# Four fused image layers on one core: channel-group means by block turns on VectorE for the later images, with new orders on all engines

## The reference, cut to what matters

```python
# L1: G = 32 groups of 4 channels, eps 1e-6;  L2: G = 16 groups of 8 channels, eps 1e-5
xg = x.reshape(B, H, W, G, C // G)
mean = jnp.mean(xg, axis=(1, 2, 4), keepdims=True)
var = jnp.var(xg, axis=(1, 2, 4), keepdims=True)
xn = (xg - mean) * jax.lax.rsqrt(var + EPS)
```

## Time and profile before

| | |
|---|---|
| median of 3 runs | 160.66 us (159.46 to 163.44) |
| the profiled execution | 159.53 us, of which the core's span is 157.7 us |
| PE, weight loads | busy 149.7 us (95%), 114.7 us (73%) |
| DVE, ACT, POOL | busy 104.8 us (66%), 108.7 us (69%), 50.1 us (32%) |
| granted clock of PE | full in all slices |

### The profile page before, as it was taken

How to read it: one execution, slowest core, us unless ns; L and a number is a source line. 1 busy time by engine, 2 the same in 40 slices (tenths; PEclk the granted TensorE clock), 3 DMA queues, 4 the chain that set the end, 5 groups by cost and what they waited for, 6 DMA issues and landing times.

```text
span 157.7 us, 3715 instructions
## 1 busy us (share of the span) xinstructions
PE 149.7 (95%) x1405; PEld 114.7 (73%) x1405; DVE 104.8 (66%) x265; ACT 108.7 (69%) x261; POOL 50.1 (32%) x115
## 2 busy tenths in 40 slices
PE   7989999999999999999989997999989999999992
PEld 4569889887777678766667765766677756799992
DVE  0577899999996898568956377639975611235543
ACT  3567979973688458983778942697358879567970
POOL 6467657534517442214020038010200050026100
PEclk9999999999999999999999999999999999999999
DMA  5960000000000000000000000000000020000003
GB/s 147 321 267 0 0 8 0 2 4 0 2 2 4 0 0 4 4 0 4 4 2 6 4 0 0 8 0 4 2 2 8 0 75 0 0 4 33 0 33 133
DMA packets 2800, 4.30 MB, mean 27 GB/s; under 512 B 352, under 2 KB 2272, under 8 KB 2784
## 3 DMA queue, kind: packets, MB, share of 16 engines
q1 hardware_dynamic: 2496, 3.87, 7.2%
q10 hardware_dynamic: 288, 0.21, 0.4%
HBM read 2.90 MB, written 1.05 MB: 25 GB/s over the span
## 4 chain that ended last, share of the span: by engine, by line
PE 71%; DVE 16%; ACT 5%; POOL 4%; issue 2%; DVEq 0%; ACTq 0%
PE psum L658 9%; PE psum L647 8%; PE psum L626 7%; DVE nmax L1148 6%; PE psum L573 4%; PE psum L553 3%; PE psum L685 3%; PE psum L699 3%; ACT pT L907 3%; PE psum L728 3%; PE psum L669 2%; PE psum L721 2%; PE psum L720 2%; PE psum L518 2%; PE psum L737 2%
## 5 line engine op out<-in xcount | busy, mean ns | idle before, releaser
L1148 DVE TENSOR_REDUCE nmax<-psum 128x4 f32<-128x1024 f32 x32 | 38.3, 1217 | 6.7 <-PE psum L626 6.7
L907 ACT ACTIVATE pT<-psum 128x1024 f32<-128x1024 f32 x32 | 31.6, 1027 | 4.7 <-PE psum L647 4.4
L626 PE MATMUL psum<-qk 16*128 16x256 f32 (+1 forms) x256 | 18.1, 397 | 0.0
L647 PE MATMUL psum<-qk 32*128 32x256 f32 (+1 forms) x256 | 18.0, 398 | 0.1
L332 POOL COPY zE<-zE 128x17 f32<-128x17 f32 x8 | 1.6, 198 | 46.1 <-ACT zE L924 46.1
L658 PE MATMUL psum<-pT,vaug_all 128*32 128x256 f32 x256 | 16.0, 383 | 0.0
L626 PEld LDWEIGHTS psum<-qk 16*128 16x128 f32 (+1 forms) x256 | 11.7, 184 | 4.4 <-DVE nmax L1148 1.5
L647 PEld LDWEIGHTS psum<-qk 32*128 32x128 f32 (+1 forms) x256 | 11.6, 184 | 3.9 <-issue 1.6
L326 POOL TENSOR_TENSOR rstd<-vare,half 128x1 f32<-128x1 f32 x16 | 9.5, 591 | 14.7 <-DVE vare L1101 14.7
L382 POOL TENSOR_SCALAR mv<-mv 128x1 f32<-128x1 f32 x16 | 6.0, 375 | 24.7 <-DVE mv L1088 24.6
L658 PEld LDWEIGHTS psum<-pT,vaug_all 128*32 128x32 f32 x256 | 7.3, 109 | 6.4 <-issue 2.2
(11 more groups left out here) (160 smaller groups left out, 352.5 us busy)
## 6 DMA issues: line engine op xcount, KB each, us to landing
out<-x SPq DMA_DIRECT2D x8, 128.0 KB, 1.9
tab<-in_weights SPq DMA_DIRECT2D x1, 708.0 KB, 7.8
tab<-in_weights SPq DMA_DIRECT2D x1, 576.0 KB, 5.4
x0T<-in_xT SPq DMA_DIRECT2D x4, 128.0 KB, 3.1
x0T<-in_xT_rest SPq DMA_DIRECT2D x1, 512.0 KB, 6.2
tab<-in_weights SPq DMA_DIRECT2D x1, 320.0 KB, 6.6
qk<-stage_all SPq DMA_DIRECT2D x16, 8.0 KB
tab<-in_weights ACTq DMA_DIRECT2D x1, 128.0 KB, 2.9
```

What stands on the lines that cost most here:

```text
L626: last = mm(bank[(b0, b1)[j // 2] + j % 2][:, u * TOK:(u + 1) * TOK], at[:, u, 0, :], at[:, :, 1, :], start=True, stop=True)
L647: last = mm(bank[(b0, b1)[j // 2] + j % 2][:, m * TOK:(m + 1) * TOK], at[:, m, 1, :], at[:, :, 0, :], start=True, stop=True)
L907: go(pT[g](i)[:, 2 * k:2 * k + 2].rearrange("p j m t -> p j (m t)"), pair(home["st", g, i][k]), ACT.Exp).then_inc(s["exp" + "EO"[g]], 1)
L1148: v.tensor_reduce(nmax2(i)[:, g, 2 * k:2 * k + 2, :], pair(home["sm", g, i][k]).rearrange("p j (u m) -> p j u m", u=TILES), AX.X, ALU.max, ...
```

## The change

For images 4 to 7 of L1 and 2 to 7 of L2 the product on PE is replaced by four DVE instructions: a turn of 32x32 blocks (`turned`), so that the 32 channels of a block lie along the columns, a sum over each 4 or 8 neighbouring columns (`group_sum`), a scaling by 1/4 or 1/8 (`group_scaled`), and a turn back of a view that repeats each result for its channels (`turned_back`). Images 0 to 3 of L1 and 0 and 1 of L2 keep the product. `mv` becomes a tile of 32 columns that GpSimd clears once. GpSimd's `x2b_out` adds the bias as a repeated tensor instead of as a per-partition scalar. All five lists of calls are in a new order, and PE's calls have other banks and marks.

```diff
+ON_PE = (4, 2)
...
-        mv = [ring(f"mv{k}", [P, 2]) for k in (1, 2)]
+        mv_all = [sb(f"mv{k}", [P, SLOTS, 32]) for k in (1, 2)]
+        mv = [lambda i, k=k: mv_all[k][:, i % SLOTS] for k in range(2)]
+        mvT, gm = ([ring(f"{n}{k}", [P, 32]) for k in (1, 2)] for n in ("mvT", "gm"))
+        sumT, gT = ([ring(f"{m}{k + 1}", [P, 32 // n]) for k, n in enumerate((GROUP1, GROUP2))] for m in ("sumT", "gT"))
...
-                gp.tensor_scalar(x2b(i), x0T(i), b_out2[:, :], None, ALU.add).then_inc(s["x2b"], 1)
+                gp.tensor_tensor(x2b(i), x0T(i), b_out2[:, :].to_broadcast((P, TOK)), ALU.add).then_inc(s["x2b"], 1)
...
+            def turned(i, layer, *marks):
+                after(marks)
+                dve.wait_ge(s[f"ms{layer}"], i + 1)
+                v.transpose(mvT[layer - 1](i), mv[layer - 1](i)).then_inc(s[f"mvT{layer}"], 1)
+            def group_sum(i, layer, *marks):
+                after(marks)
+                dve.wait_ge(s[f"mvT{layer}"], nth(i, layer))
+                n = (GROUP1, GROUP2)[layer - 1]
+                v.tensor_reduce(sumT[layer - 1](i), mvT[layer - 1](i).rearrange("p (k n) -> p k n", n=n), AX.X, ALU.add).then_inc(s[f"sumT{layer}"], 1)
+            def group_scaled(i, layer, *marks):
+                after(marks)
+                dve.wait_ge(s[f"sumT{layer}"], nth(i, layer))
+                n = (GROUP1, GROUP2)[layer - 1]
+                v.tensor_scalar(gT[layer - 1](i), sumT[layer - 1](i), 1.0 / n, None, ALU.mult).then_inc(s[f"gT{layer}"], 1)
+            def turned_back(i, layer, *marks):
+                after(marks)
+                dve.wait_ge(s[f"gT{layer}"], nth(i, layer))
+                n = (GROUP1, GROUP2)[layer - 1]
+                v.transpose(gm[layer - 1](i), gT[layer - 1](i).unsqueeze(2).to_broadcast((P, 32 // n, n))).then_inc(s[f"gm{layer}"], 1)
...
-                dve.wait_ge(s[f"gm{layer}"], i + 1)
-                g = bank[home[f"o{layer - 1}", i]][:, TOK:TOK + 2]
+                if i < ON_PE[layer - 1]:
+                    dve.wait_ge(s[f"gp{layer}"], i + 1)
+                else:
+                    dve.wait_ge(s[f"gm{layer}"], nth(i, layer))
+                g = group(i, layer)
...
-            x2_out(4); moments(4, 2); nmax2_out(2, 1, 1); oinv_out(0); p0_scaled(7); on_out(0); mean(4, 2)
...
+            turned(2, 2); group_sum(2, 2); group_scaled(2, 2); turned_back(2, 2); variance(2, 2); variance_eps(2, 2)
```

More of the change, by code:

```diff
@@ L301, in fill @@
                 gp.memset(gw_all[:, :, :, :], 0.0).then_inc(s["filled"], 1)
+                for k in range(2):
+                    gp.memset(mv_all[k][:, :, :], 0.0)
                 gp.memset(stage_all[:, :, 1, :], 1.0)
@@ L524, in gm1 @@
                 pe.wait_ge(s["ms1"], i + 1)
-                mm(bank[home["o0", i]][:, TOK:TOK + 2], w("mean1"), mv[0](i), start=True, stop=True).then_inc(s["gm1"], 1)
+                mm(bank[home["o0", i]][:, TOK:TOK + 2], w("mean1"), mv[0](i)[:, 0:2], start=True, stop=True).then_inc(s["gp1"], 1)
             def qk1(i, b, *marks):
@@ L591, in gm2 @@
                 pe.wait_ge(s["ms2"], i + 1)
-                mm(bank[home["o1", i]][:, TOK:TOK + 2], w("mean2"), mv[1](i), start=True, stop=True).then_inc(s["gm2"], 1)
+                mm(bank[home["o1", i]][:, TOK:TOK + 2], w("mean2"), mv[1](i)[:, 0:2], start=True, stop=True).then_inc(s["gp2"], 1)
             def qk2(i, b, *marks):
@@ new lines, in _ @@
+            pv(0, 0, 2, ("stage", 2)); st(1, 1, 4, 0, ("nmaxE", 5)); ot(0, 2); qk2(3, 3)
+            st(1, 0, 6, 4, ("nmaxE", 6), ("expO", 3)); o0(6, 2, ("on", 1)); gwm(7, 0, ("expO", 4)); x2t(0, 1)
+            p0t(7, 2, ("x1", 7)); ont(0); p1t(5, 6, ("expE", 3)); o0(7, 2); v2m(2, 0); o2(0, 1)
+            sm(3, 1, 6, 2, ("p1T", 6), ("x1", 8)); qk1(6, 1, ("x3", 1)); v1m(6, 4, ("expE", 4)); o1(5, 5)
+            s1(6, 0, ("vaug", 3)); sm(3, 0, 2, 6, ("nmaxO", 8)); nt(2, 4, ("v1", 7)); qk2(4, 1)
@@ new lines, in _ @@
+            x2t(3, 1, ("on", 4)); nt(7, 0, ("on", 5)); x2t(4, 3); ont(3); st(6, 1, 6, 4, ("expE", 14)); ont(4)
+            o2(3, 2, ("oTO", 6)); v2m(7, 1); zm(2, 0); st(7, 0, 2, 6, ("onT", 5), ("x3", 4)); pv(6, 0, 0, ("z", 3))
+            zm(3, 1); st(7, 1, 2, 4, ("expE", 15)); ym(1, 1, ("z", 4)); o2(4, 6, ("expE", 16)); am(2, 7)
+            am(3, 2, ("expO", 15)); om(0, 6, ("x3", 5)); pv(6, 1, 3); pv(7, 1, 6, ("xout", 1))
+            pv(7, 0, 0, ("oTE", 7)); zm(4, 6, ("oTO", 8)); ot(5, 7); ym(2, 0, ("oTE", 8)); ot(6, 6, ("z", 5))
@@ L1108, in normalised @@
                 k = layer - 1
[L1109 to L1110 removed]
+                v.tensor_scalar(xn[k](i), x0T(i), group(i, layer)[:, 0:1], rstd[k](i), ALU.subtract, ALU.mult
                                 ).then_inc(s[f"xn{layer}"], 1)
@@ new lines, in _ @@
+            variance_eps(6, 2); moments(7, 2); normalised(6, 2); mean(7, 2); oinv_out(2); turned(7, 2)
+            group_sum(7, 2); group_scaled(7, 2); turned_back(7, 2); variance(7, 2); variance_eps(7, 2); on_out(2)
+            normalised(7, 2, ("v2", 5)); nmax2_out(6, 0, 0); nmax2_out(6, 0, 1); nmax2_out(6, 1, 0)
+            nmax2_out(6, 1, 1); nmax2_out(7, 1, 0); nmax2_out(7, 1, 1); x3_out(2); nmax2_out(7, 0, 0)
+            nmax2_out(7, 0, 1); oinv_out(3); oinv_out(4); on_out(3); on_out(4); x3_out(3); x3_out(4); a_out(2); xo(0)
```

248 lines of the change are left out of this document (122 added, 126 removed).

## The result

The changed kernel takes 160.44 us (median of 20 runs, 159.9 to 162.1); the kernel before, run beside it on the same chip, 159.53 us (20 runs). The ratio is 1.0053, 95% interval 1.0032 to 1.0074: slower by half a per cent, where 158.0 us had been forecast. The range (154.6 to 161.9) holds it, but the sign is wrong.

The account below looks back on a forecast made before the run. PE working through its queue in order was taken as the bound, with DVE the path in one stretch; -2.2 - 0.4 + 1.5 + 0.5 - 1.0 - 0.5 = -2.1 gave 157.4, with a margin 158.0 us, range 154.6 to 161.9.

Parts of the forecast that it names:

- Ten products go, -2.2: On PE's queue: ten mean products removed at a mean 0.22 us each, -2.2 us (bounds -1.5 and -3.1).
- their waits, -0.4: On PE: idle weight loads before the removed products, waiting for GpSimd's squares, a third of 1.2 us counted, -0.4 us.
- the products were a fill: Second rival: PE waits elsewhere for what it no longer does, DVE's lateness eats every term; 160.1 us, chance 0.20.
- Forty instructions at 0.20: On DVE's queue: forty new dependent instructions at 0.20 us each (bounds 0.10 and 0.33), 8.0 us of DVE.
- DVE late at image 3, +1.5: At the maxima of image 3's odd heads: PE asks earlier, DVE arrives late, +1.5 us (bounds 0 and +5.6).
- the other sixteen, +0.5: Remaining 16 new DVE instructions: idle time hides them but not the longer way to the normalised image, +0.5 us.
- The wait for zsum, -1.0: PE's 1.02 us wait before image 1's first folded product goes as GpSimd's new order brings zsum earlier, -1.0 us.
- x2b at nothing: GpSimd's x2b as two-tensor operation: eight times 0.23 us shorter, but counted as nothing for the total.
- The front, -0.5: First 33 us: later images' work between dependent steps cuts PE's 2.0 us idle time, -0.5 us (bounds 0 and -1.0).
- the margin for a median of 160.66 us over three runs: Added to the 157.4 us sum: half of the 1.1 us by which that median exceeded the profiled execution, giving 158.0.
- A path along DVE for 30 us or more: Sign to check in the new profile: if the path runs that long on DVE, the +1.5 us was too small.
- The third rival: DVE becomes the bound from 30 to 66 us, an image costs 1.8 us instead of 0.8; 164.1 us, chance 0.11.

Follow-up runs that it names:

- none_old: Kernel before, old orders and old x2b, ten products left out with nothing in their place (no group averaging for those images): 158.98 us, ratio 0.9950.
- none_new: Changed kernel without its forty new DVE instructions, group averaging left out for the ten images: 158.32 us, ratio 0.9898.
- fill_new: none_new with one small unread sum, waiting for nothing, at each of the forty places of the new DVE instructions: 158.51 us, ratio 0.9918.
- x2b_old: Kernel before with one line changed, GpSimd's x2b in the two-tensor form: 158.77 us, ratio 0.9948.
- zsum_old: x2b_old with zsum of image 1 moved on GpSimd to right behind its wrap, ahead of a square and two x2b: 158.93 us, ratio 0.9949.
- x2b_back: Changed kernel with x2b back in its one-input form: 160.33 us, ratio 1.0030.
- swap_old: Kernel before, old orders and old x2b, with the swap alone: ten products replaced by four DVE instructions per image: 164.76 us, ratio 1.0308.
- best_old: zsum_old with three x2b moved behind image 5's score shift and one DVE maximum moved behind image 6's layer 2 normalisation: 161.45 us, ratio 1.0075.
- late_old: x2b_old with the swap for images 5 to 7 of layer 2 alone: 160.80 us, ratio 1.0066.

## Why the prediction was wrong, step by step

**Ten products go, -2.2, and their waits, -0.4.** This step failed most. none_old puts the two together at -0.5. The price of one product (0.22 us start to start) was right, as none_old's busy time shows; the inference that work taken off PE's queue comes off the time was not. The text leaned on 0.1 us of idle time for PE in that stretch while it also said, from the earlier trace rows, that PE's records there are what DVE lets through. The second reading was the true one: of the 1.9 us of busy time that PE lost in none_old, 1.2 came back as idle time. The text named this as a rival, that the products were a fill, at 160.1 us and a chance of 0.20. That is what happened in half of the mechanism: the products were a fill, but what ate the gain was not only DVE's lateness at image 3; part of it was gone before any turn was added.

**Forty instructions at 0.20.** Right: 205, 185, 162 and 210 ns each, and 0.21 us from one dependent step to the next.

**DVE late at image 3, +1.5, and the other sixteen, +0.5.** Together 2.0; the forty cost 2.1 in these orders. The size is right, and so is the place: laid over none_new, the changed kernel is 1.8 us later at the first maximum of image 3 and loses 0.75 more behind it. The reason is right only in part. The text charged DVE's queue time net of what had been moved behind image 3, and expected PE to ask for that maximum early and DVE to be late with it. fill_new has forty instructions at the same places and loses 0.2 to 0.8 us, so most of the price needs the waits between the steps. And PE did not ask early. PE's row of that score product and DVE's row behind it, in the changed kernel:

```profile
68.78 1.15 PE psum L632 x16
```

```profile
69.99 1.23 DVE L1192 TENSOR_REDUCE nmax<-psum 128x4 f32<-128x1024 f32 x1
```

The maxima start at 69.99 us, right behind the product: DVE is not late for PE there. PE starts the product at 68.78, not at the 64.6 that the shorter queue promised. In none_new it starts at 67.75, so most of the missing 4.2 us has nothing to do with the forty steps: of the 9.0 us of work taken out of PE's queue ahead of it 4.8 came off the time, against the 73.6 of before. 2.4 us of the rest is idle time of PE in this stretch; where the remainder went no row shows.

**The wait for zsum, -1.0.** The wait is gone from the changed kernel as said. In the orders of before 0.7 us of it could be had: x2b_old gets that by shortening the wait, and zsum_old hardly more by removing it, since the wait for the normalisation of image 6 stood right behind. The term was 0.3 us too high, and it did not ask what is late next.

**x2b at nothing.** Half right. In the new orders it is worth nothing (x2b_back). In the old ones it is worth 0.7 us, through the zsum wait, which the sum had booked under the orders. The instructions take 0.61 us by the median and 665 ns on average in the changed kernel, against 952 on average before. The chances hold 0.04 for a two-input x2b that is dearer than the one-input one; no run shows such a price, and in the traces the two-input form is the shorter.

**The front, -0.5.** Nothing to be seen: PE is idle 2.45 us ahead of 33.2, against 2.0. Executions differ by more than that in the first 31 us: the 128x512 maximum from which the traces are laid over each other starts at 30.5 to 31.7 us.

**The sum** as the runs have it: products -0.5, x2b or the orders in its place -0.7, forty instructions +2.1, together +0.9; measured +0.91. In the prediction it was -2.1. Another 0.6 us of the forecast's level was the margin for a median of 160.66 us over three runs; over twenty the kernel before takes 159.53. That the range held the result is owed to its width, not to the mechanism.

Of the signs named ahead: the mean lines show 12 records, the turns 0.21 us, DVE 111.5 us busy, the zsum wait gone, all as said. The last two sets of score products start at 126.3 and 129.0 us, not at 125. Image 3's maxima start at 69.99 us, not at 66 to 68, and DVE is busy 84% of the time up to them, not close to 90%. PE is idle 3.8 us between 33 and 130, just under the 4 that would have called the forecast wrong. "A path along DVE for 30 us or more would mean that +1.5 was too small": the chain has 30% of 158.6, so 48 us, on DVE (25 us before), and that sign was the right one to watch.

**The third rival** (DVE the bound, 1.8 us per image, slower by 4.6) came nearest in swap_old: in the orders of before the swap costs 5.3 us, of which about 4.4 are its own. Its profiled execution has

```profile
14.00:16.00 2.00, 2.00 (x11) 1.86 (x11) 1.23 (x5) 1.82 (x6) 1.64 (x5) 0.66 0.00 0
16.00:18.00 2.00, 2.00 (x9) 1.85 (x8) 1.44 (x6) 1.24 (x5) 1.13 (x2) 0.50 0.00 0
```

a granted clock of 0.66 and 0.50, ahead of the first turn, after PE had been busy 1.46 and 1.89 us of the two times two before; by its first maximum of 128x1024 it is 1.5 us later than the kernel before (34.70 us, 33.23). What the prediction never priced is the swap in the orders of before, and so how much of what the new orders give it would use up.

Left open: what the new orders would make with the products kept. It wasn't tried, since the banks that the products need are reused earlier in these orders.

## What to carry to other kernels

Price a replacement by the dependent steps that it puts between two queues before the engine time that it takes or frees: forty free instructions cost 0.2 us here, forty chained ones 2.1, and ten products off the busiest engine gave 0.5. Lay traces over each other from an instruction ahead of the first difference, since two executions of the same work were up to 1.2 us apart there. Before booking a removed wait in full, look what the same engine would have waited for next. And when a swap comes with new orders, ask what each is worth alone; here the swap alone cost 4.4 us or more, and the orders paid back a good part of it.

## What the runs showed of the hardware

- A low granted clock stood behind a stretch in which PE was less busy, in some executions. In best_old's trace PE was busy 0.59 of 2 us, and the granted clock then fell to 0.50 and 0.72 for four microseconds; in late_old's 2.69 of 4 us busy were followed by 0.58. No run shows that the one brings the other: in the trace of the kernel before PE was busy 1.55 and 1.43 of two times 2 us from 94 to 98 us, and the clock was 1.00 in both and in the one behind them. Five of best_old's twelve executions and seven of late_old's keep a mean clock of 1.00, and the changed kernel's profiled execution does too.
- DVE's normalisation (128x256, two per-partition operands) took 0.41 to 0.42 us by the median of all sixteen (before, x2b_old), 0.57 beside GpSimd's one-input x2b in two cases of three in the kernel before (0.41 in the third) and 0.69 beside the two-tensor one. Moving x2b away brought both from 0.69 to 0.42 and gave 0.4 us in the old orders; in the new ones a like move gave 0.2, which is not clear of noise.
- Small DVE instructions that wait for nothing started 0.12 to 0.13 us apart, each lasting 0.21 (four sums at 48.22 in fill_new); ones that wait for the last started 0.21 to 0.25 apart (four steps of image 2, layer 2, in the changed kernel).
- A block turn of 128x32 took 205 to 210 ns on average in the changed kernel, against 185 ns for the sum and 162 for the scaling.
